# Experts with stacked high and low parts, resident weights and a second product two steps behind

## The reference

```python
xn = _layernorm(x, ln_gamma, ln_beta)
logits = einsum('bnd,des->bnes', l2norm(xn) * scale, l2norm(mu))   # E = 16 experts, S = 16 slots
dispatch = softmax(logits, axis=1)
combine = softmax(logits.reshape(B, N, E * S), axis=-1).reshape(B, N, E, S)
slot_in = einsum('bnd,bnes->besd', xn, dispatch)
h = gelu(einsum('besd,edh->besh', slot_in, w1) + b1[None, :, None, :])   # 256 -> 64
slot_out = einsum('besh,ehd->besd', h, w2) + b2[None, :, None, :]        # 64 -> 256
out = einsum('besd,bnes->bnd', slot_out, combine)
```

## Time and profile before

| | us |
|---|---|
| median of 3 runs | 1213.59 (1213.54 to 1218.73) |
| the profiled execution | 1216.6 |
| its span, first to last instruction | 1214.8 |
| PE busy | 1047.5 (86%) |
| DVE busy | 894.0 (74%) |
| ACT busy | 734.7 (60%) |
| POOL busy | 439.4 (36%) |
| mean granted clock of PE | 0.925 |

### The profile page before, as it was taken

One profiled execution on the slowest core, in us unless ns is written; L12 is line 12 of the kernel. 1 busy time (PEld: TensorE's weight loads), 2 busy tenths in 40 slices (PEclk: granted clock), 3 DMA queues, 4 the chain that ended last, 5 costly groups with the idle time before them and its releaser, 6 DMA issues. The chain is left out here.

```text
span 1214.8 us, 28495 instructions
## 1 busy us (share of the span) xinstructions
PE 1047.5 (86%) x8053; PEld 998.5 (82%) x8053; DVE 894.0 (74%) x2324; ACT 734.7 (60%) x2481; POOL 439.4 (36%) x753
## 2 busy tenths in 40 slices
PE   6779999999999998799999917888888657777998
PEld 6679999999999998799999916888778646777777
DVE  3567667777767775677777647899998579996656
ACT  3466666676666665433333318899999346666754
POOL 0222323222232321121212126667776457663015
PEclk9889999999999999899999967899999769989559
DMA  7678970000000000000000045555664100000113
GB/s 223 144 134 227 130 117 0 0 0 0 0 0 0 0 1 1 31 1 0 0 0 0 0 108 150 150 159 161 175 172 128 19 1 1 0 0 2 42 35 121
DMA packets 71574, 73.90 MB, mean 61 GB/s; under 512 B 23024, under 2 KB 63828, under 8 KB 71380
## 3 DMA queue, kind: packets, MB, share of 16 engines
q1 hardware_dynamic: 70692, 72.47, 24.3%
q10 hardware_dynamic: 816, 0.66, 0.2%
HBM read 41.52 MB, written 31.54 MB: 60 GB/s over the span
## 5 line engine op out<-in xcount | busy, mean ns | idle before, releaser
L776 POOL TENSOR_TENSOR att_prob<-att_ex,att_rinv 128x308 f32<-128x308 f32 x128 | 90.0, 703 | 215.8 <-DVE att_rinv L679 202.5
L1056 ACT ACTIVATE att_ex<-att_s_bank,att_mx 128x77 f32<-128x77 f32 x512 | 144.3, 347 | 14.2 <-DVE att_mx L1122 12.7
L1338 ACT ACTIVATE ffn_hid<-ffn_h_bank,ffn_b 128x256 f32<-128x256 f32 x128 | 60.8, 476 | 125.5 <-DVE ffn_hT_lo L1369 64.8
L638 ACT ACTIVATE att_ex<-att_s_bank,att_mx 128x77 f32<-128x77 f32 x512 | 125.1, 333 | 11.5 <-DVE att_mx L669 11.4
L702 DVE TENSOR_TENSOR att_pT_lo<-att_t_bank,att_pT_hi 128x512 fp32r<-128x512 f32 x128 | 88.3, 690 | 33.2 <-ACT att_pT_hi L616 32.9
L646 ACT ACTIVATE att_qT<-att_q_bank 128x256 f32<-128x256 f32 x128 | 49.2, 385 | 100.3 <-PE att_q_bank L496 99.1
L1196 POOL TENSOR_TENSOR att_prob<-att_ex,att_rinv 128x256 f32<-128x256 f32 x128 | 80.3, 628 | 72.1 <-DVE att_rinv L1137 72.0
L516 PE MATMUL att_s_bank<-att_keys,att_qT 128*128 128x154 f32 x512 | 95.1, 309 | 0.0
L616 ACT CAST att_pT_hi<-att_t_bank 128x512 fp32r<-128x512 f32 x128 | 75.0, 587 | 24.6 <-PE att_t_bank L526 19.8
L540 PE MATMUL att_o_bank<-att_pT_hi,att_vals_hi 128*128 128x256 f32 x256 | 83.0, 324 | 3.0 <-DVE att_oT_lo L683 2.0
L1309 PE MATMUL ffn_o_bank<-ffn_w_hi,ffn_hT_hi 128*128 128x256 f32 x256 | 74.4, 291 | 7.6 <-DVE ffn_hT_lo L1369 7.6
(11 more groups left out here) (275 smaller groups left out, 4162.6 us busy)
## 6 DMA issues: line engine op xcount, KB each, us to landing
att_qs<-q_dram SPq DMA_DIRECT2D x96, 128.0 KB, 2.8
ks_dram<-att_zeros SPq DMA_DIRECT2D x16, 462.0 KB, 5.7
att_ks<-ks_dram SPq DMA_DIRECT2D x16, 462.0 KB, 5.0
all_x<-in_x SPq DMA_DIRECT2D x4, 1024.0 KB, 7.1
att_vd<-vd_dram SPq DMA_DIRECT2D x16, 256.0 KB
q_dram<-att_qT_hi SPq DMA_DIRECT2D x16, 256.0 KB, 2.1
q_dram<-att_qT_lo SPq DMA_DIRECT2D x16, 256.0 KB, 2.1
out<-comb_y SPq DMA_DIRECT2D x16, 256.0 KB, 2.1
```

What stands on the lines that cost most here:

```text
L638: last = nc.scalar.activation(ex[t % RING][:, r, :], s_bank[t % 2][:, r * SK:(r + 1) * SK], ACT.Exp, bias=mx[t % 2][:, r:r + 1])
L776: nc.gpsimd.tensor_tensor(out, e, w, ALU.mult).then_inc(p_ready, 1)
L1056: last = nc.scalar.activation(ex[t % RING][:, r, :], s_bank[t % 2][:, r * SK:(r + 1) * SK], ACT.Exp, bias=mx[t % 2][:, r:r + 1], **total)
```

## The change

- Weights: all of w1 and w2 are loaded into SBUF while routing runs, w2 twice, into partitions 0 to 63 and 64 to 127. The biases b1 are loaded twice as well. No transfer is left in the expert phase.
- `up` uses w1 with its 64 columns repeated, so that the result stands twice, in rows 0 to 63 and 64 to 127 of PSUM. Gelu is made on 128 rows.
- The hidden values are kept in one tile: the high part in the lower 64 rows, the low part in the upper 64. One matmul with the doubled w2 over 128 rows makes high-high and high-low in one pass, a second one over 64 rows makes low-high. `down` has four matmuls instead of six.
- The split of w1 (two casts, two subtractions of 128 x 128) and the subtraction of w2 (64 x 256) move to POOL. ACT still casts w2, now over 128 rows.
- `down` runs two steps behind `up`, with three buffers for w2 and the hidden values. The steps are all written out instead of a loop, and the waits are for constants.

```diff
@@ -1497,11 +1497,13 @@
-            sp.dma_start(st.b_raw[:, 0:HID], d["L1_ffn_b1"]).then_inc(expert_in, 16)
-            sp.dma_start(st.b_raw[:, HID:], d["L1_ffn_b2"]).then_inc(expert_in, 16)
-            for i in range(2):
-                load_expert(sp, d, st, i, i, expert_in)
-            sp.wait_ge(expert_in, 96)
+            for h in range(2):
+                sp.dma_start(st.b_raw[:, h * HID:(h + 1) * HID], d["L1_ffn_b1"]).then_inc(expert_in, 16)
+                sp.dma_start(st.w2_raw[h * HID:(h + 1) * HID, :, :], d["L1_ffn_w2"].rearrange("e h n -> h e n")).then_inc(expert_in, 16)
+            sp.dma_start(st.b_raw[:, 2 * HID:], d["L1_ffn_b2"]).then_inc(expert_in, 16)
+            for c in range(DC):
+                sp.dma_start(st.w1_raw[:, c, :, :], d["L1_ffn_w1"][:, c * P:(c + 1) * P, :].rearrange("e p h -> p e h")).then_inc(expert_in, 16)
+            sp.wait_ge(expert_in, 112)
...
@@ -1776,146 +1778,153 @@
 def experts(nc, d, st):
 
+    LAG, RING = 2, 3
     with ExitStack() as stack:
         m = Memory(nc, stack, "exp")
-        b1, b2 = m.sb("b1", [HID, E]), m.sb("b2", [P, DC, E])
+        b1, b2 = m.sb("b1", [P, E]), m.sb("b2", [P, DC, E])
         w1_raw, w2_raw, b_raw = st.w1_raw, st.w2_raw, st.b_raw
-        w1 = [m.split(f"w1_{i}", [P, DC, HID]) for i in range(2)]
-        w2 = [m.split(f"w2_{i}", [HID, D]) for i in range(2)]
+        w1 = [m.split(f"w1_{i}", [P, DC, 2, HID]) for i in range(2)]
+        w2 = [m.split(f"w2_{i}", [P, D]) for i in range(RING)]
         xin = [m.split(f"xin{i}", [P, DC, B, S]) for i in range(2)]
-        hid = [m.sb(f"hid{i}", [HID, B * S]) for i in range(2)]
-        hT = [m.split(f"hT{i}", [HID, B * S]) for i in range(2)]
+        hid = [m.sb(f"hid{i}", [P, B * S]) for i in range(2)]
+        hT = [m.sb(f"hT{i}", [P, B * S], F32R) for i in range(RING)]
         b_bank = m.ps("b_bank")
         h_bank = [m.ps(f"h_bank{i}") for i in range(2)]
...
-        w_in = [m.sem(f"w_in{i}") for i in range(2)]
-        in_hi, in_lo, w2_hi, w2_lo = m.sem("in_hi"), m.sem("in_lo"), m.sem("w2_hi"), m.sem("w2_lo")
+        in_hi, in_lo = m.sem("in_hi"), m.sem("in_lo")
+        w1_hi, w1_lo, w2_hi, w2_lo = m.sem("w1_hi"), m.sem("w1_lo"), m.sem("w2_hi"), m.sem("w2_lo")
...
         def slots_of(e):
-            return st.slots[:, :, :, bass.ds(e * S, S)]
...
+            return st.slots[:, :, :, e * S:(e + 1) * S]
+
+        def w1_of(e):
+            return w1_raw[:, :, e, :].unsqueeze(2).to_broadcast([P, DC, 2, HID])
 
         @block.tensor
+            def up(e):
+                i = e % 2
+                pe.wait_ge(w1_lo, e + 1)
                 pe.wait_ge(in_lo, e + 1)
...
+                    last = nc.tensor.matmul(h_bank[i][:, 0:B * S], w1[i][a][:, c, :, :], xin[i][b][:, c, :, :],
                                             start=n == 0, stop=n == 5)
...
+            def down(e):
+                i, r = e % 2, e % RING
+                pe.wait_ge(w2_lo, e + 1)
                 pe.wait_ge(hid_lo, e + 1)
-                pe.wait_ge(w2_lo, e + 1)
                 at_least(pe, out_stored, DC * (e - 1))
                 for c in range(DC):
-                    for n, (a, b) in enumerate(PASSES):
-                        last = nc.tensor.matmul(o_bank[i][:, c * B * S:(c + 1) * B * S], w2[i][a][:, c * P:(c + 1) * P],
-                                                hT[i][b][:, :], start=n == 0, stop=n == 2)
+                    out = o_bank[i][:, c * B * S:(c + 1) * B * S]
+                    nc.tensor.matmul(out, w2[r][0][:, c * P:(c + 1) * P], hT[r][:, :], start=True, stop=False)
+                    last = nc.tensor.matmul(out, w2[r][1][0:HID, c * P:(c + 1) * P], hT[r][0:HID, :], start=False, stop=True)
                 last.then_inc(o_psum, 1)
 
...
+            nc.tensor.transpose(b_bank[:, 0:E], b_raw[:, 0:P], st.ident[0:E, 0:E])
...
+            for e in range(E + LAG):
+                if e < E:
+                    up(e)
+                if e >= LAG:
+                    down(e - LAG)
 
         @block.scalar
         def _(act):
+            def round_inputs(e):
                 at_least(act, h_psum, e - 1)
-                nc.scalar.copy(w1[i][0][:, :, :], w1_raw[i][:, :, :])
...
+                nc.scalar.copy(xin[e % 2][0][:, :, :, :], slots_of(e)).then_inc(in_hi, 1)
+
+            def round_w2(e):
+                at_least(act, o_psum, e - 2)
+                nc.scalar.copy(w2[e % RING][0][:, :], w2_raw[:, e, :]).then_inc(w2_hi, 1)
+
+            def hidden(e):
+                act.wait_ge(h_psum, e + 1)
+                at_least(act, hid_lo, e - 1)
+                nc.scalar.activation(hid[e % 2][:, :], h_bank[e % 2][:, 0:B * S], ACT.Gelu,
+                                     bias=b1[:, e:e + 1]).then_inc(hid_ready, 1)
+
+            def outputs(e):
+                act.wait_ge(o_psum, e + 1)
+                act.wait_ge(in_lo, e + 1)
+                for c in range(DC):
+                    nc.scalar.activation(st.slots[:, c, :, e * S:(e + 1) * S],
+                                         o_bank[e % 2][:, c * B * S:(c + 1) * B * S].rearrange("p (b s) -> p b s", b=B),
+                                         ACT.Identity, bias=b2[:, c, e:e + 1]).then_inc(out_stored, 1)
+
+            round_inputs(0)
             act.wait_ge(b_ready, 2)
-            batch_pairs(act, step)
+            for e in range(E + LAG):
+                if e + 1 < E:
+                    round_inputs(e + 1)
+                if e < E:
+                    hidden(e)
+                    round_w2(e)
+                if e >= LAG:
+                    outputs(e - LAG)
 
         @block.vector
         def _(dve):
+            def split_inputs(e):
                 dve.wait_ge(in_hi, e + 1)
+                for c in range(DC):
+                    last = nc.vector.tensor_tensor(xin[e % 2][1][:, c, :, :], st.slots[:, c, :, e * S:(e + 1) * S],
+                                                   fp32_of(xin[e % 2][0][:, c, :, :]), ALU.subtract)
                 last.then_inc(in_lo, 1)
 
+            def split_hidden(e):
+                r = e % RING
+                dve.wait_ge(hid_ready, e + 1)
+                at_least(dve, o_psum, e - 2)
+                nc.vector.tensor_copy(hT[r][:, :], hid[e % 2][:, :]).then_inc(hid_hi, 1)
+                dve.wait_ge(hid_hi, e + 1)
+                nc.vector.tensor_tensor(hT[r][HID:P, :], hid[e % 2][HID:P, :], fp32_of(hT[r][HID:P, :]), ALU.subtract).then_inc(hid_lo, 1)
+
+            split_inputs(0)
...
+            nc.vector.tensor_copy(b1[:, :], b_bank[:, 0:E]).then_inc(b_ready, 1)
...
+            for e in range(E):
+                if e + 1 < E:
+                    split_inputs(e + 1)
+                split_hidden(e)
+
+        @block.gpsimd
+        def _(pool):
+            def split_w1(e):
+                i = e % 2
+                at_least(pool, h_psum, e - 1)
+                for c in range(DC):
+                    hi = nc.gpsimd.tensor_copy(w1[i][0][:, c, :, :], w1_of(e)[:, c, :, :])
+                hi.then_inc(w1_hi, 1)
+                pool.wait_ge(w1_hi, e + 1)
+                for c in range(DC):
+                    lo = nc.gpsimd.tensor_tensor(w1[i][1][:, c, :, :], w1_of(e)[:, c, :, :], fp32_of(w1[i][0][:, c, :, :]), ALU.subtract)
+                lo.then_inc(w1_lo, 1)
+
+            def split_w2(e):
+                r = e % RING
+                pool.wait_ge(w2_hi, e + 1)
+                nc.gpsimd.tensor_tensor(w2[r][1][0:HID, :], w2_raw[0:HID, e, :], fp32_of(w2[r][0][0:HID, :]), ALU.subtract).then_inc(w2_lo, 1)
+
+            split_w1(0)
+            for e in range(E):
+                if e + 1 < E:
+                    split_w1(e + 1)
+                split_w2(e)
@@ -2026,9 +2035,9 @@
         m = Memory(nc, stack, "moe")
         st.slots = m.sb("slots", [P, DC, B, ES])
         st.comb = m.sb("comb", [P, EC, B, N])
-        st.w1_raw = [m.sb(f"w1_raw{i}", [P, DC, HID]) for i in range(2)]
-        st.w2_raw = [m.sb(f"w2_raw{i}", [HID, D]) for i in range(2)]
-        st.b_raw = m.sb("b_raw", [E, HID + D])
+        st.w1_raw = m.sb("w1_raw", [P, DC, E, HID])
+        st.w2_raw = m.sb("w2_raw", [P, E, D])
+        st.b_raw = m.sb("b_raw", [E, P + D])
```

More of the change, by code:

```diff
@@ L1807, in slots_of @@
         def slots_of(e):
-            return st.slots[:, :, :, bass.ds(e * S, S)]
[L1810 to L1815, removed]
+            return st.slots[:, :, :, e * S:(e + 1) * S]
+        def w1_of(e):
+            return w1_raw[:, :, e, :].unsqueeze(2).to_broadcast([P, DC, 2, HID])
         @block.tensor
         def _(pe):
-            def up(e, i):
+            def up(e):
+                i = e % 2
+                pe.wait_ge(w1_lo, e + 1)
                 pe.wait_ge(in_lo, e + 1)
@@ L1822, in up @@
                 for n, (c, (a, b)) in enumerate((c, ab) for c in range(DC) for ab in PASSES):
-                    last = nc.tensor.matmul(h_bank[i][0:HID, 0:B * S], w1[i][a][:, c, :], xin[i][b][:, c, :, :],
```

(34 more changed lines are left out.)

5 lines of the change are left out of this document (removed).

## The result

The changed kernel is slower: 1226.42 us against 1217.67 us for the one before (medians of 8 runs each), ratio 1.007 with a 95% interval of 1.005 to 1.0091. The forecast was 1206.8 us, 6.8 us taken off a median of 1213.59 that the larger set of runs moved to 1217.67; the range ended at 1213.5. The profiled span is 1221.2 us, 6.4 us over the 1214.8 of before. All of it lies in the expert phase: `combine` begins at 1179.95 instead of 1173.57, 6.4 us later, and takes as long as before.

The account below looks back on a forecast made before the run. PE at its low clock was taken to set the 3.07 us step. Steps 13 x (3.07 - 2.60) = 6.1, minus 3 x 0.3, plus 0.6 and 1.0, gain 6.8 us: 1213.59 to 1206.8 us, range 1201 to 1213.5.

Parts of the forecast that it names:

- PE's term: PE in an expert step: ten matmuls, 2.15 us, plus 0.58 for block changes, 2.73 us at the lower clock.
- The loop through all engines: Dependence loop through ACT, DVE and PE over two steps: 2.48 us a step at the upper clock, 2.90 at the lower.
- I expect the clock to rise after about three steps: PE clock in the expert phase: rises to near 1.00; three slower steps before that cost 3 x 0.3 us.
- The clock stays low: Rival, chance 0.18: expert phase stays at clock 0.50, step 2.90 us, gain 3.3 us, time 1210.3 us.
- Forecast 2.6 us a step: POOL's period in the expert phase with its five new instructions, bounds 2.4 and 3.1 us.
- the growth by collisions: POOL's added time from meeting four DVE operations a step: 0.3 us taken, from 0.12 to 0.76.
- The rival of full exclusion: Rival, chance 0.12: DVE's operations add wholly to POOL's in the expert phase, 3.7 us a step, time 1220.8 us.
- Head and tail: Expert phase ends: 0.6 us gained ahead of expert 2, 1.0 us gained behind the last `up`.
- Transfers and ACT: Weight loads moved into routing priced at nothing; ACT needs 2.0 us an expert step and is no bound.
- The 70 us for loading: Loading about 3 MB of weights during routing at 43 GB/s, within routing's over 140 us.

Follow-up runs that it names:

- e7: Kernel before, with only the third matmul of each half of `down` over 128 zero-filled rows, four row changes a step instead of two; ratio 1.0095 to before.
- e10: Changed kernel with `down` sorted, both 128-row matmuls first, and the w2 subtraction moved from POOL back to DVE; ratio 0.9934 to the kernel before.
- e1: Changed kernel with the low-high matmul of `down` over all 128 rows, unused rows zeroed once, so no row changes; ratio 0.995 to the kernel before.
- e9: Changed kernel with only the subtraction of w2 moved from POOL back to DVE; ratio 1.0072 to the kernel before.
- e8: e1 slowed by one more addition on POOL a step, result unused; run once, step 3.41 us.
- e3: Changed kernel with `down` one step behind `up` instead of two, and rings of two; ratio 1.0045 to the kernel before.
- e4: Kernel before with all w1 and w2 resident, loaded during routing, and split where they were; ratio 1.0004 to the kernel before.
- e6: Kernel before with all six matmuls of `down` over 128 rows, the upper 64 zeroed once; ratio 0.9978 to the kernel before.

## Why the prediction was wrong

**PE's term.** The step that failed: "That makes 0.12 + 0.17 + 0.12 + 0.17 = 0.58, so PE needs 2.73 us." I took the gaps of the earlier trace rows for the price of a change of block and counted two. They are the price of a change between 128-row and 64-row weights, and the new `down` has two more of them inside, where I put 0.215. The sum is 1.2, not 0.58, and PE needs 3.32 us. The distances in the changed kernel and in e7, and the step of e10, show the price; e1 shows no price for a change of block; e9 shows that POOL does not set the step. Why a change stops the early load of weights stays open; all 64-row weights here lie in rows 0 to 63, and no run placed them elsewhere. The earlier trace rows could have told: they show the gaps only where rows change, and none of my rows shows a change of block without one. The loop through all engines (2.90 us at the lower clock) holds the same gaps and lacks the two in `down` as well.

**The loads of weights.** In the timelines of the changed kernel and of e7 the next weights load beside a running matmul of equal rows (PEld at 1145.48 above), and do not at a change between 128 and 64 (PEld at 1146.04). The Trainium skill's page "TensorE: Matmul & The Clock Gate" (Part 3, The mechanism) says that weight loads overlap with running matmuls only when the row group differs. The trace disagrees with that sentence for these shapes: the rows of both are equal where the load overlaps, matmuls of equal rows start 0.21 us apart, and 0.51 where the rows change on both sides. The same section of that page of the Trainium skill also lets a load into the background weight buffer go ahead of running matmuls; which buffer a load takes, no row here shows.

**The clock.** "I expect the clock to rise after about three steps" failed too. In the changed kernel it is 0.50 with PE busy 10.00 of 10 us, as before. e9 and e10 differ only in the order and banks of `down`, four changes against two, and the clock of 1140 to 1150 us is 0.50 and 0.81; e8 shows that the absence of changes is not enough. The rival "The clock stays low" had its condition fulfilled, yet its 1210.3 us missed by 16: its 2.90 us a step left out the same changes.

**POOL.** Forecast 2.6 us a step, and 2.69 in e1, where it is the bound; the growth by collisions was 0.5 us instead of 0.3. In the changed kernel it lies behind PE. The rival of full exclusion, slower than before, had the right sign and the wrong cause: POOL idles 3 of 10 us. Even in e1 its 3.7 us a step did not come, and the loss was shared: POOL's step grew by 0.5 us and each of DVE's two input subtractions by 0.15.

**Head and tail.** Forecast 0.6 and 1.0 us gained. The head lost 0.6 (expert 2 starts 7.98 instead of 7.35 us after the phase's first work, waiting for POOL's first splits). The tail lost 3.0: three second products stand behind each other at 2.04 us (4 x 0.51), where the lag of one has two; I had counted its chain of dependences, not PE's queue. e3 puts the lag's part at 1.8 us, and 1.2 is left for what a second product takes longer than before. Together: 13 x 0.25 + 0.6 + 3.0 is 6.9 us, less 0.45 by which the phase began earlier in this execution, is the 6.4 measured.

**Transfers and ACT.** Transfers were priced at nothing, and e4 confirms it for the kernel before. The 70 us for loading were far off: the 3 MB were through some 17 us after the first was issued (966 to 983 us), with 213 GB/s from 970 to 980 us instead of 43, which was only what the expert phase asked for, 64 KB at a time. ACT had 6.38 us of 10 and bounded nothing.

## What to carry to other kernels

Count how often neighbouring matmuls change between 128 and 64 rows of weights, not only how many there are: here a pass saved by stacking was worth 0.21 us and each change it brought 0.30. Filling the unused rows with zeros once kept the loads of weights ahead, and its cost does not show in the times; sorting the matmuls by rows did about as well (0.997 against 0.995, and 0.9934 against 0.992, with intervals that overlap). A longer lag puts another block into the drain on the engine that is busiest. Look again at what was free: once PE got faster, POOL (e1) and the weights' loads (e6) were the next bounds.

## What the runs showed of the hardware

At the lower clock (1.2 GHz) one change between 128-row and 64-row weights cost 0.30 us in the changed kernel and in e7, and 0.19 in the kernel before where 128-row weights of only 64 columns follow; at the upper (2.4 GHz) it was about 0.19 in e10. Matmuls of equal rows, 64 or 128, started 0.21 us apart at the lower clock, and those of 128 rows 0.12 at the upper. A change from 128 to 64 columns at equal rows cost nothing in e7. PE can be shown as busy 10.00 of 10 us while it starts 31 matmuls instead of 41.
